# Where GpSimd adds the output bias to x in a two-stage graph kernel: in front of or behind its scaling of the attention probabilities

## The reference

```python
def attention_layer(x):                       # 8 heads of 32
    q, k, v = split_heads(x @ Wq.T + bq), split_heads(x @ Wk.T + bk), split_heads(x @ Wv.T + bv)
    scores = where(mask, q @ k.T * SCALE, -1e9)   # 6 static masks, 2 from adj
    return merge(softmax(scores) @ v) @ Wo.T + bo

def graph_layer(h):                           # 4 heads
    Wh = h @ W.T + bW
    A = tanh(where(adj, (Wh @ attn) @ Wh.T, 0))
    ha = concat(relu(A @ Wh)) @ A_w.T
    hf = h @ fc_w.T
    c = sigmoid(hf @ g1_w.T + ha @ g2_w.T + gbias)
    return hf * c + ha * (1 - c)

h = layernorm(x + attention_layer(x))
out = layernorm(h + graph_layer(h))
```

## Time and profile before

| | |
|---|---|
| runs | 1244.65, 1247.8 and 1253.7 us; median 1247.8 |
| profiled execution | 1256.22 us, of which the span is 1254.4 us |
| mean granted clock of TensorE | 0.966 of full speed |
| busy | TensorE 92%, VectorE 58%, ScalarE 41%, GpSimd 19% |
| DMA | 26 GB/s over the span |

### The profile page before, as it was taken

The page is one execution under the profiler, slowest core; times in us unless marked ns, Lnnn a source line. Parts: engine busy times, 40 slices in busy tenths (PEclk is TensorE's granted clock), DMA queues, the critical chain, the costliest instruction groups (busy, mean ns, idle before and its releaser), DMA issues.

```text
span 1254.4 us, 24543 instructions
## 1 busy us (share of the span) xinstructions
PE 1156.9 (92%) x9756; PEld 939.7 (75%) x9756; DVE 723.7 (58%) x1321; ACT 511.4 (41%) x910; POOL 240.9 (19%) x230
## 2 busy tenths in 40 slices
PE   5789989999899999989999998999999899998886
PEld 5667868788786878878687787878778787877765
DVE  6345565656556575655657565565756556574533
ACT  3535343443534344353534435343443534344241
POOL 1321121312112131212213121121312122130100
PEclk8789999999999999999999999999999999998898
DMA  6000001010000101000010100001010000100000
GB/s 210 20 19 20 19 18 38 17 37 17 19 18 17 37 17 37 17 19 18 17 37 17 36 17 19 18 17 37 17 37 17 19 18 17 37 18 2 1 17 17
DMA packets 26699, 32.58 MB, mean 26 GB/s; under 512 B 4400, under 2 KB 23344, under 8 KB 26288
## 3 DMA queue, kind: packets, MB, share of 16 engines
q1 hardware_dynamic: 26672, 32.19, 7.8%
HBM read 23.80 MB, written 8.39 MB: 26 GB/s over the span
## 4 chain that ended last, share of the span: by engine, by line
PE 87%; issue 4%; DVE 4%; ACT 3%; SPq 0%; DMA 0%; POOL 0%; POOLq 0%; DVEq 0%; ACTq 0%
PE bankB L329 18%; PE bankB L330 17%; PE bankB L331 17%; PE bankB L508 6%; PE bankA L329 5%; PE bankB L524 5%; PE bankA L330 5%; PE bankA L331 5%; PE bankA L424 3%; PE bankA L449 2%; ACT U_hi L725 1%; PE bankB L570 1%; PE bankA L475 1%; PE bankA L435 1%; ACT PT L686 1%
## 5 line engine op out<-in xcount | busy, mean ns | idle before, releaser
L731 ACT ACTIVATE cat_hi<-bankB 128x512 fp32r<-128x512 f32 x128 | 76.5, 598 | 134.7 <-PE bankB L331 134.7
L801 DVE SCALAR_TENSOR_TENSOR cat_lo<-bankB,cat_hi 128x512 fp32r<-128x512 f32 x128 | 86.4, 685 | 55.1 <-ACT cat_hi L731 54.1
L801 DVE SCALAR_TENSOR_TENSOR U_lo<-bankB,U_hi 128x512 fp32r<-128x512 f32 x128 | 79.5, 683 | 63.0 <-ACT U_hi L725 63.0
L329 PE MATMUL bankB<-hT_lo,g_hi 128*128 128x512 f32 x256 | 108.7, 425 | 0.0
L703 ACT ACTIVATE T<-bankB 128x512 f32<-128x512 f32 x128 | 75.4, 589 | 78.2 <-PE bankB L331 78.2
L329 PE MATMUL bankB<-U_lo,wt_hi 128*128 128x512 f32 x256 | 102.9, 402 | 3.7 <-DVE U_lo L801 2.3
L330 PE MATMUL bankB<-U_hi,wt_lo 128*128 128x512 f32 x256 | 101.4, 396 | 0.0
L331 PE MATMUL bankB<-U_hi,wt_hi 128*128 128x512 f32 x256 | 101.3, 396 | 0.0
L330 PE MATMUL bankB<-hT_hi,g_lo 128*128 128x512 f32 x256 | 101.0, 394 | 0.0
L331 PE MATMUL bankB<-hT_hi,g_hi 128*128 128x512 f32 x256 | 100.1, 391 | 0.0
L329 PE MATMUL bankB<-cat_lo,aw_hi 128*128 128x512 f32 x256 | 99.6, 389 | 0.0
(11 more groups left out here) (141 smaller groups left out, 2663.7 us busy)
## 6 DMA issues: line engine op xcount, KB each, us to landing
x_raw<-in_xT SPq DMA_DIRECT2D x16, 512.0 KB, 3.3
y<-in_x SPq DMA_DIRECT2D x16, 512.0 KB, 3.6
out<-res SPq DMA_DIRECT2D x16, 512.0 KB, 3.0
W_nat<-in_Wn SPq DMA_DIRECT2D x1, 1028.0 KB, 5.9
adjS_u<-in_adjS SPq DMA_DIRECT2D x32, 32.0 KB, 2.8
attn_nat<-in_attn SPq DMA_DIRECT2D x1, 1024.0 KB, 8.0
raw_A<-in_AwT SPq DMA_DIRECT2D x1, 1024.0 KB, 10.0
adjT_u<-in_adjT SPq DMA_DIRECT2D x16, 32.0 KB, 2.8
```

Source lines behind the costliest of these rows:

```text
L329: pe.matmul(out, asel(a[0]), bsel(b[1]), start=first, stop=False)
L731: act.activation(cat_hi[:, n, :], bank[:], ACT.Relu).then_inc(cat_hi_ready, 1)
L801: return dve.scalar_tensor_tensor(out=out, in0=bank, scalar=bias, in1=hi.bitcast(F32), op0=op, op1=ALU.subtract)
```

## The change

The add of the bias becomes a function of its own, `x_and_bias`. For group 0 it is called where the add was. In every other turn it is called behind `probs_scaled(A)`, so that GpSimd first scales the four parts of the probabilities and then adds bo to x. No other engine's program changes.

```diff
-            def probs_scaled(g):
+            def x_and_bias(g):
                 if not later(g):
                     pool.wait_ge(rows_in, 16 * 2)
                 pool.wait_ge(x_in, g * 16 + 16)
                 pool.tensor_tensor(y[:], y[:], bo_all[:, 0:D].unsqueeze(1).to_broadcast([P, NP, D]), ALU.add) \
                     .then_inc(xb_ready, 1)
+
+            def probs_scaled(g):
                 for j in range(JB):
                     pool.wait_ge(den_ready, g * JB + (j + 1))
...
                 if B is None:
                     mask(0)
+                    x_and_bias(0)
                     probs_scaled(0)
...
                 if A is not None:
                     probs_scaled(A)
+                    x_and_bias(A)
                 if more:
                     x_low(A + 1)
```

## The result

The changed kernel takes 1208.74 us at the median of four runs (1207.26 to 1214.99); the kernel before took 1250.19 at the median of four, the three given above and one of 1252.58. The ratio is 0.9682, 95% interval 0.9629 to 0.9735: 3.2% faster. The forecast was 1214 us, range 1204 to 1229. The profiled execution took 1207.26 us, span 1205.4, and the mean granted clock went from 0.966 to 0.986.

What follows compares the result with a forecast made beforehand. TensorE, busy 1156.9 of 1254.4 us, bounds the kernel, so only idle and slow-clock time can go: 27.7 us of stall plus 13.5 of clock falls, 41.2 off 1256.2, gives 1215.0; 1214 taken, range 1204 to 1229.

Steps and rivals of the forecast that it cites:

- What the stall was: TensorE's 1.97 us stall before L508: last T copy waits behind ScalarE's fourth exp, VectorE's softmax and L988, held by GpSimd's add.
- Rival 3: At L508: the stall is TensorE's own issue (fetching its program), so the change does nothing; 1247.8 us, chance 0.06.
- 2.07 us for the softmax chain: On VectorE: without the add beside it the first L988 takes 0.406 instead of 2.473 us, so softmax starts 2.07 us sooner.
- 27.7 us of stall: In front of L508: 13 stalls of 1.97 us gone, and 2.07 us off the one in the last overlapped turn.
- The slack of 0.11 us: At L508: the last T copy arrives by 683.55, TensorE is busy until 683.66, so the stall goes with 0.11 us spare.
- rival 2: Before L508: another chain step takes the stall over; half of stall and falls stay, 1235.6 us, chance 0.08.
- The clock: At L508: 8 falls of TensorE's clock behind the stalls, 1.69 us each, 13.5 us, expected gone with the stall.
- Rival 1: On TensorE: the clock's falls stay or move to attention's stalls; 1228.5 us if 8 stay, chance 0.10.
- The collision at L907: At VectorE's masked product: the add in its new place holds it, put at 1.5 us and hidden.
- The cover: Between the masked product's end and TensorE's first gather (L524): 3.5 us left, enough to hide the held product.
- The time: Whole kernel: 41.2 us off the profiled 1256.2 gives 1215.0; 1214 us taken.
- the alternative that the prediction names: Whole kernel: if the 8.4 us between median and profiled run are something else that stays off, 1206.6 us.

Runs made afterwards that it cites:

- the doses: Changed kernel with half the add, a memset, or unused adds of 1024 or 1536 elements beside L988: 1226.1, 1227.0, 1234.0, 1261.2 us.
- the first experiment: Changed kernel with the add moved in front of root_2, beside VectorE's gate (L976, L979): 1222.86 us, ratio 0.9805 to the kernel before.

## Why the prediction was right

The steps in its own order:

- **What the stall was.** Shown: with L988 held but the T copy ahead of the exp the stall is gone; with L988 free it is gone too; with something else beside L988 it is back. Rival 3 (TensorE's own issue) falls with the first of these.
- **2.07 us for the softmax chain.** The longest L988 fell from 2473 to 414 ns, by 2.06 us, and a turn of the loop without a fall from 72.5 to 70.5 us, as forecast. 27.7 us of stall were to go; of the 27.8 us of the earlier trace rows 0.1 are left.
- **The slack of 0.11 us.** The stalls say 0.08 us, the turns' lengths 0.02 or less. The step that I had called thin held, and with next to nothing to spare: had the chain been a few tenths of a us longer, rival 2 would have had its share. That it was not is partly luck.
- **The clock.** All 8 falls went, 13.5 us; the middle stretch with 7 of them lost 40.4 us, where 27.8 + 7 x 1.69 = 39.6 was the sum; the other 0.8 us are not accounted for. Rival 1 (the falls move to attention) didn't come: the granted clock of the middle stretch is 1.00. That they hang on the stall is shown by the runs of the first point, in which the falls go with the stall whether L988 is held or not, and by the doses: none of 42 stalls of 0.9 to 1.7 us brought one, 8 of 14 at 2.0 and 9 of 14 at 2.35.
- **The collision at L907.** Put at 1.5 us, measured 1947 - 693 = 1.25 us, and hidden. The cover was put at 3.5 us; unheld, the product would end at 662.97, 3.35 us ahead of the gather. The Trainium skill, "SBUF — State Buffer", SBUF: two separate sides, has the lock follow the add to any VectorE instruction with two SBUF inputs; the trace agrees, at L907 here and at L979 in the first experiment (2.79 us).
- **The time.** 41.2 us were forecast and the medians differ by 41.5. The 5 us between 1214 and 1208.7 come from where the sum was made: I had read the 8.4 us by which the profiled execution lay over the median as five falls of the clock behind L508, and took most of that for lost already. The changed kernel has no such falls, and its runs are spread just as wide (1205.66 to 1216.39). So a spread of that size needs no falls behind L508; in the profiles of all these kernels it lies at the start (the first L508 at 92.06 to 98.69 us) and behind the last overlapped L508 (117 to 128 us). 1247.8 - 41.2 = 1206.6, the alternative that the prediction names, was the better base. How many falls the kernel before had in its other runs is not known.

## What to carry to other kernels

An instruction on an engine with 20% load and no dependency on the busy chain can still set the end, by standing in the way of another engine's short instruction. Look for a line whose longest instance is as long as some GpSimd instruction, and move that GpSimd instruction beside something that has slack or doesn't mind; beside the gate it would have lost over a third of the gain. And where the chain of waits names nobody, look at the in-order queue of the engine that should have released the semaphore: here two different edits, on two engines, took away the same stall.

## What was not expected of the hardware

- A GpSimd memset, which reads nothing, holds VectorE's one-input SBUF instruction as an add does (1378 and 1441 ns). This one was expected, but it had not been measured.
- How long a held instruction lasts depends on its kind. A held L988 (one input in SBUF) ends 0.14 or 0.15 us behind the GpSimd instruction in each of these profiles, a held L907, L976 or L979 (two inputs in SBUF) 0.54 to 0.55 us behind it, whatever holds it and for how long.
- The one that waits gets the next turn. Between two GpSimd adds issued back to back a held VectorE instruction ran, and the second add was 0.49 us longer (2.86 against 2.37 us), in two kernels: in the one above with 1536 elements in the new place, and in the first experiment, where the gate's L976 ran between the sum of hT and the add.
- Not every VectorE instruction is held. In the turn of the changed kernel shown above, GpSimd makes x's low half, until 685.39, while VectorE adds the projection from PSUM to y (L945, 0.69 us) and begins the first of four moments (L934, 0.43 us; the three behind it, with GpSimd idle, take 0.41). Neither is held. GpSimd, then VectorE:

```profile
682.98 2.41 POOL L1039 TENSOR_TENSOR x_lo<-x_raw,x_hi 128x1024 fp32r<-128x1024 f32 x1 [19.30 <-ACT x_hi L624]
```

```profile
684.23 0.69 DVE L945 TENSOR_TENSOR y<-bankA,y 128x512 f32<-128x512 f32 x1 [0.75 <-PE bankA L331]
685.03 1.41 DVE L934 BATCH_NORM_STATS2 stats<-y 128x6 f32<-128x256 f32 x4
```

- In these executions the drop of TensorE's clock behind a stall looks like a step and not like a slope: nothing up to 1.70 us, more than half of the turns from 1.97 us, 1.69 us each time. It cost 13.5 of the 41 us here.
